# Four chained convolution blocks on one core: image 0 loaded in whole rows, weights loaded later, idle memsets left out in two images, and a new order of work

## What is computed

```python
# L0: bottleneck with a deformable convolution
mid    = relu(bn1(conv1x1(x, conv1_w)))             # 512 -> 128 channels
offset = conv3x3(mid, off_w) + off_b                # 18 channels: 9 taps, 2 coordinates
hid    = relu(bn2(deform_conv3x3(mid, offset, conv2_w)))
x      = relu(bn3(conv1x1(hid, conv3_w)) + x)       # 128 -> 512
# L1: local self correlation, 25 shifts, normalised, joined to x
corr   = l2norm(self_correlation(x, 5))
x      = relu(conv1x1(concat(x, corr), W) + b)
# L2 and L3: two plain bottlenecks 512 -> 128 -> 3x3 -> 512 with residual
```

## Time and profile before

| what | value |
|---|---|
| median of three executions | 602.6 us |
| the profiled execution's own time | 605.4 us |
| its span, from first to last instruction | 603.6 us |
| TensorE busy, share of the span | 562.2 us, 93% |
| VectorE busy | 442.3 us, 73% |
| GpSimd busy | 409.5 us, 68% |
| ScalarE busy | 327.3 us, 54% |
| mean granted TensorE clock | 0.976 of full |

### The profile page before, as it was taken

The page is one execution under the profiler, slowest core; times in us unless marked ns, Lnnn a source line. Parts: engine busy times, 40 slices in busy tenths (PEclk is TensorE's granted clock), DMA queues, the critical chain, the costliest instruction groups (busy, mean ns, idle before and its releaser), DMA issues.

```text
span 603.6 us, 8850 instructions
## 1 busy us (share of the span) xinstructions
PE 562.2 (93%) x2550; PEld 416.9 (69%) x2550; DVE 442.3 (73%) x1277; ACT 327.3 (54%) x718; POOL 409.5 (68%) x718
## 2 busy tenths in 40 slices
PE   9478986699999999799999999999999999999996
PEld 4434753576777777469777777688777776987774
DVE  3447789798988788689986788998884674463444
ACT  3445756446654874555645857654557633433534
POOL 2388888888888898888888888888787300003060
PEclk9888998899999999899999999999999999999999
DMA  8898997964568555866586557856765213000003
GB/s 307 286 355 292 276 366 222 310 186 143 160 193 296 165 150 162 280 205 171 168 264 204 168 168 251 251 159 175 223 183 148 72 59 134 0 1 1 1 1 139
DMA packets 48034, 110.08 MB, mean 182 GB/s; under 512 B 7655, under 2 KB 15911, under 8 KB 47858
## 3 DMA queue, kind: packets, MB, share of 16 engines
q0 software_dynamic: 23040, 75.52, 41.8%
q1 hardware_dynamic: 22274, 32.59, 15.6%
q10 hardware_dynamic: 2672, 1.41, 0.8%
HBM read 96.94 MB, written 12.55 MB: 181 GB/s over the span
## 4 chain that ended last, share of the span: by engine, by line
PE 71%; POOL 18%; DVE 4%; issue 3%; DMA 2%; ACT 1%; POOLq 0%; DVEq 0%; ACTq 0%
PE bank L630 16%; PE bank L632 16%; PE bank L631 16%; POOL patch L597 14%; PE bank L741 7%; POOL tick L602 4%; PE bank L749 4%; PE bank L818 4%; PE bank L730 4%; DMA patch<-patch_tables,idx_all 2%; PE bank L787 1%; PE bank L666 1%; PE bank L653 1%; DVE samp L1189 1%; DVE ring L1250 1%
## 5 line engine op out<-in xcount | busy, mean ns | idle before, releaser
L1189 DVE SCALAR_TENSOR_TENSOR samp<-patch,wgt_all,samp 128x128 f32<-128x128 f32 x864 | 240.7, 347 | 22.7 <-ACT samp L911 20.1
L597 POOL DMA_INDIRECT patch<-patch_tables,idx_all x216 | 219.8, 1017 | 40.2 <-DVE samp L1189 10.7
L911 ACT ACTIVATE samp<-patch,wgt_all 128x128 f32<-128x128 f32 x288 | 102.0, 396 | 76.4 <-DMA patch<-patch_table,idx_all 35.3
L597 POOL DMA_INDIRECT patch<-patch_table,idx_all x72 | 70.5, 980 | 30.9 <-DVE far L1086 20.3
L613 POOL TENSOR_TENSOR kept<-xs_high,xs_low 128x512 f32<-128x512 f32 x12 | 16.5, 1405 | 100.3 <-PE bank L632 100.3
L602 POOL TENSOR_TENSOR tick<-tick 1x1 f32<-1x1 f32 x288 | 79.7, 277 | 5.0
L741 PE MATMUL bank<-sampT,w 128*128 128x512 f32 x144 | 71.9, 606 | 1.5 <-ACT sampT L919 1.5
L730 PEld LDWEIGHTS bank<-ident_r,samp 128*128 128x128 f32 x288 | 35.8, 144 | 31.4 <-DVE samp L1189 16.8
L919 ACT ACTIVATE sampT<-bank 128x512 f32<-128x512 f32 x72 | 41.9, 591 | 27.8 <-PE bank L730 26.8
L730 PE MATMUL bank<-ident_r,samp 128*128 128x128 f32 x288 | 44.1, 280 | 10.5 <-DVE samp L1189 10.5
L630 PE MATMUL bank<-x_high,l1w_high 128*128 128x512 f32 x128 | 53.9, 421 | 0.0
(11 more groups left out here) (187 smaller groups left out, 1203.1 us busy)
## 6 DMA issues: line engine op xcount, KB each, us to landing
x_whole<-in_x SPq DMA_DIRECT2D x32, 256.0 KB, 7.2
out_y<-ring SPq DMA_DIRECT2D x32, 256.0 KB, 3.3
xa<-in_x SPq DMA_DIRECT2D x6, 1024.0 KB, 8.5
patch<-patch_tables,idx_all POOLq DMA_INDIRECT x216, 3.5
patch_tables<-midT SPq DMA_DIRECT2D x11, 256.0 KB, 7.1
xa<-in_x SPq DMA_DIRECT2D x8, 256.0 KB, 5.7
patch<-patch_table,idx_all POOLq DMA_INDIRECT x72, 6.0
l1w_whole<-in_l1wt SPq DMA_DIRECT2D x1, 1024.0 KB, 10.4
```

The source lines that it names most:

```text
L597: pool.indirect_dma_start(patch[:, n % SLOTS].rearrange("p a c -> p (a c)"), None, patches_n if i else patches_0, bass.IndirectOffsetOnAxi ...
L911: act.activation(samp[:, n % SAMPS, t, :], patch[:, g % SLOTS, 0, :], ACT.Copy, scale=wgt_all[:, i, (HT * h + t) * TAPS + k, 0:1]).then_in ...
L1189: dve.scalar_tensor_tensor(o_, g_, w_, o_, ALU.mult, ALU.add).then_inc(blended, 1)
```

## The change

1. **x of image 0** comes as 4 DMAs of 512 KB with whole rows of 1024 pixels, straight into x_whole, where the residual is kept. conv1 of image 0 reads it there, chunk by chunk, both halves after each other for a chunk; the 8 res loads of image 0 are gone. x of later images comes in two pieces by channel groups, and no longer by halves; image 1's is issued at once, behind image 0's.
2. **Start.** TensorE's matmuls on zeros are one of 512 and one of 256 columns, for three of 512. It waits for w1 alone, and not for the parameters too. VectorE makes its constants before it waits for the parameters.
3. **Weights.** Each waits on SP for a turn of image 0: WEIGHT_PACE gives the unit, X_PACE that of later x loads. w2 and w3 wait for image 0's table only.
4. **Pauses** are 0 in images 0 and 1, and 2 in images 2 and 3. (Before they were 0 in image 0 too.)
5. **Tables.** Each image has its own tensor in DRAM.
6. **ORDER** is a new list of 1548 steps. It differs nearly everywhere.

```diff
-PAUSE, PAUSES = 120, 2
+PAUSE, PAUSES = 120, (0, 0, 2, 2)
...
-conv1.0.0 conv1.0.1 mid.0.0 taps.0.0 mid.0.1 taps.0.2 tapped.0.0 taps.0.1 tapped.0.2 midT.0.0 tapped.0.1 midT.0.1
+conv1.0.0 conv1.0.1 mid.0.0 taps.0.0 mid.0.1 taps.0.1 tapped.0.0 taps.0.2 tapped.0.1 midT.0.1 tapped.0.2 midT.0.0
...
+WEIGHT_PACE = {7: 1, 2: 2, 3: 2, 4: 3, 5: 3, 0: 4, 1: 4, 6: 7}
+X_PACE = {2: 0, 3: 5}
...
-    table_0 = nc.dram_tensor("patch_table_0", (HW, 2 * P), fp32, kind="Internal")
-    table_n = nc.dram_tensor("patch_tables", ((N - 1) * HW, 2 * P), fp32, kind="Internal")
+    tables = [nc.dram_tensor(f"patch_table_{i}", (HW, 2 * P), fp32, kind="Internal") for i in range(N)]
...
             def load_x(i, h):
-                sp.dma_start(xa[:, :, h * HALF:(h + 1) * HALF],
-                             x_v[i, :, :, h * HALF:(h + 1) * HALF]).then_inc(ld_xa[h], 16)
+                some = slice(h * KC // 2, (h + 1) * KC // 2)
+                sp.dma_start(xa[:, some, :], x_v[i, :, some, :]).then_inc(ld_xa[h], 16)
...
+            for k in range(KC):
+                sp.dma_start(whole["x1"][:, k, PADK:PADK + H, :], grid_rows(x_v[0, :, k, :])).then_inc(ld_x0[k], 16)
             for h in range(2):
-                for k in range(KC):
-                    cols = slice(h * HALF, (h + 1) * HALF)
-                    sp.dma_start(xa[:, k, cols], x_v[0, :, k, cols]).then_inc(ld_x0[h][k], 16)
...
+                load_x(1, h)
...
+                    sp.wait_ge(conv1_done, nth(("conv1", i - 1, 0), ("conv1", i - 1, 1)))
+                    sp.wait_ge(turned, nth(("turn", 0, X_PACE[i] + h)))
                     load_x(i, h)
+                elif it[0] == "ldw":
+                    n = it[1]
+                    if n in WEIGHT_PACE:
+                        sp.wait_ge(turned, nth(("turn", 0, WEIGHT_PACE[n])))
+                    else:
+                        sp.wait_ge(tabled[0], table_dmas(0))
...
-                        for _ in range(PAUSES if i and t == HT - 1 else 0):
+                        for _ in range(PAUSES[i] if t == HT - 1 else 0):
...
             pe.wait_ge(zeroed, 1)
-            for _ in range(3):
-                pe.matmul(bank[TURN_BANK][:], w3_s[:, 0:P], w3_s[:], start=True, stop=True)
-            pe.wait_ge(ld_first, 32)
+            for n in (C, C // 2):
+                pe.matmul(bank[TURN_BANK][:, 0:n], w3_s[:, 0:P], w3_s[:, 0:n], start=True, stop=True)
+            pe.wait_ge(ld_w1, 16)
...
+                        elif h == 0:
+                            pe.wait_ge(ld_x0[c], 16)
+                            for half in range(2 if c < KC - 1 else 1):
+                                last = pe.matmul(first[half][:], w1[:, c, :], residual(half, c),
+                                                 start=c == 0, stop=c == KC - 1)
```

More of the change, by code:

```diff
@@ L44 @@
 ORDER = """
-conv1.0.0 conv1.0.1 mid.0.0 taps.0.0 mid.0.1 taps.0.2 tapped.0.0 taps.0.1 tapped.0.2 midT.0.0 tapped.0.1 midT.0.1
-pixels.0.0 shift.0 pixels.0.1 table.0.0 table.0.1 scale.0 scale.1 index.0 gather.0.0.0 hats.0 turnw.0 positions.0
-turnw.1 split.1 gather.0.0.1 split.4 split.3 split.5 gather.0.1.0 weigh.0.0.0 splitlow.5 blend.0.0.0 gather.0.1.1
-weigh.0.0.1 w3turn conv1.1.1 blend.0.0.1 xload.1.0 gather.0.2.0 weigh.0.1.0 gather.0.2.1 turn.0.0 xload.2.1 w3scale
-gather.0.3.0 split.2 mid.1.1 split.0 splitlow.0 weigh.0.1.1 sampT.0.0 blend.0.1.0 conv1.1.0 gather.0.3.1 weigh.0.2.0
@@ L65 @@
-gather.0.13.1 xsum.0.0.2 tap.0.9 positions.2 blend.0.12.0 table.3.0 res.0.1.3 res.0.1.1 out0.0.0.1 taps.3.0
-weigh.0.12.1 xsum.0.0.1 blend.0.12.1 gather.0.14.0 xhigh.0.0.0 sampT.0.11 sampT.0.10 xhigh.0.0.3 weigh.0.13.0
-xhigh.0.0.1 xlow.0.0.1 xlow.0.0.3 gather.0.14.1 xlow.0.0.0 blend.0.13.0 weigh.0.13.1 tapped.3.0 gather.0.15.0
-tapped.3.2 blend.0.13.1 shift.3 weigh.0.14.0 blend.0.14.0 gather.0.15.1 weigh.0.14.1 xhigh.0.0.2 blend.0.14.1
-gather.0.16.0 turn.0.12 tap.0.10 tap.0.11 sampT.0.12 xlow.0.0.2 weigh.0.15.0 index.3 blend.0.15.0 tap.0.12
@@ new lines @@
+pixels.0.1 shift.0 pixels.0.0 table.0.1 table.0.0 index.0 ldw.8 gather.0.0.0 hats.0 conv1.1.1 positions.0 ldw.9
+gather.0.0.1 gather.0.1.0 weigh.0.0.0 w3turn conv1.1.0 mid.1.1 blend.0.0.0 mid.1.0 gather.0.1.1 taps.1.1 taps.1.2
+tapped.1.2 weigh.0.0.1 blend.0.0.1 gather.0.2.0 turn.0.0 midT.1.1 w3scale weigh.0.1.0 midT.1.0 taps.1.0 blend.0.1.0
+gather.0.2.1 weigh.0.1.1 blend.0.1.1 gather.0.3.0 turn.0.1 weigh.0.2.0 tapped.1.0 weigh.0.2.1 sampT.0.0 blend.0.2.0
+gather.0.3.1 ldw.7 xload.2.1 pixels.1.1 sampT.0.1 tapped.1.1 blend.0.2.1 gather.0.4.0 turn.0.2 weigh.0.3.0 tap.0.0
@@ new lines @@
+ldw.2 xload.2.0 blend.0.3.0 tap.0.1 w3back shift.1 ldw.3 gather.0.4.1 weigh.0.3.1 w3s blend.0.3.1 gather.0.5.0
+weigh.0.4.0 blend.0.4.0 index.1 gather.0.5.1 weigh.0.4.1 turn.0.3 conv1.2.1 gather.0.6.0 blend.0.4.1 weigh.0.5.0
+blend.0.5.0 gather.0.6.1 ldw.4 split.4 sampT.0.2 weigh.0.5.1 blend.0.5.1 ldw.5 table.1.1 split.3 hats.1 gather.0.7.0
+turn.0.4 conv1.2.0 ldw.0 weigh.0.6.0 sampT.0.3 gather.0.7.1 mid.2.1 ldw.1 blend.0.6.0 positions.1 weigh.0.6.1 mid.2.0
+midT.2.1 tap.0.2 turn.0.5 blend.0.6.1 splitlow.3 taps.2.2 gather.0.8.0 midT.2.0 split.2 sampT.0.4 pixels.2.1
@@ new lines @@
+tapped.2.2 weigh.0.7.0 pixels.1.0 splitlow.2 turn.0.6 tap.0.3 gather.0.8.1 xload.3.0 table.1.0 weigh.0.7.1 taps.2.1
+taps.2.0 tap.0.4 blend.0.7.0 sampT.0.6 sampT.0.5 gather.0.9.0 xload.3.1 tapped.2.0 scale.1 blend.0.7.1 tapped.2.1
+split.5 pixels.2.0 weigh.0.8.0 turn.0.7 gather.0.9.1 turnw.1 shift.2 tap.0.5 ldw.6 weigh.0.8.1 scale.0 split.1
+blend.0.8.0 bias splitlow.1 gather.0.10.0 blend.0.8.1 weigh.0.9.0 sampT.0.7 blend.0.9.0 gather.0.10.1 tap.0.6 turn.0.8
+sampT.0.8 tap.0.7 index.2 splitlow.4 split.6 weigh.0.9.1 tap.0.8 conv1.3.0 gather.0.11.0 weigh.0.10.0 hid.0.0
@@ new lines @@
+blend.0.9.1 gather.0.11.1 blend.0.10.0 splitlow.6 out0.0.0.0 weigh.0.10.1 hats.2 out0.0.0.3 gather.0.12.0 turn.0.9
+turnw.0 out0.0.0.2 split.0 weigh.0.11.0 xsum.0.0.3 mid.3.0 blend.0.10.1 gather.0.12.1 xhigh.0.0.3 sampT.0.9
+weigh.0.11.1 xlow.0.0.3 xsum.0.0.2 xsum.0.0.0 conv1.3.1 midT.3.0 turn.0.10 blend.0.11.0 gather.0.13.0 weigh.0.12.0
+blend.0.11.1 corrw gather.0.13.1 blend.0.12.0 splitlow.0 turn.0.11 mid.3.1 xhigh.0.0.0 gather.0.14.0 splitlow.5
+out0.0.0.1 taps.3.0 sampT.0.10 pixels.3.0 xhigh.0.0.2 weigh.0.12.1 gather.0.14.1 taps.3.2 tap.0.9 midT.3.1 taps.3.1
@@ L450, in table_dmas @@
         def table_dmas(image):
-            return 16 * (5 if image < 2 else 4)
+            return 16 * 5
         def finals(it):
```

383 lines of the change are left out of this document (185 added, 198 removed).

## The result

The change makes the kernel slower: 607.84 us median (603.24 to 613.92, 20 runs) beside 602.84 us for the kernel before on the same chip (20 runs), ratio 1.0074 with a 95% interval of 1.0052 to 1.0096. The forecast was 597.3 us, range 593 to 603.5.

What follows compares the result with a forecast made beforehand. GpSimd's image 0 gathers bound the kernel to about 137 us, then TensorE, except a stall near 250 us. Terms −0.9 + 0.5 − 6.0 + 1.0 = −5.4 us took the profiled 605.4 to 600.0, given as a 597.3 us median, range 593 to 603.5.

Steps and rivals of the forecast that it cites:

- Start, −0.9 us: Up to the first gather: shorter zeros and earlier x let conv1 end 0.9 us sooner, bounds 0 and 1.7 us.
- rival for a cold start: conv1 begins at half clock and ends at 14.2 to 15.1 us; total 598.3 to 599.1 us; chance 0.06.
- Image 0's samples, +0.5 us: Image 0's 72 gathers: 2.6 us more VectorE work mostly fits its idle time, costing 0.5 us; GpSimd unchanged.
- The stall, −6.0 us: Near 250 us: without image 1's pauses, TensorE's 4.2 us wait and 1.8 us of half-clock loss go.
- What is late next, +1.0 us: Image 1's first third: denser VectorE work makes new waits of 1.0 us, bounds 0 and 6.
- I take 0 for the new order: Said of the tail: same chain of cvB, ex, add and store, so the new order costs 0.
- Signs: Expected profile marks; wrong if TensorE idles over 10 us after 138 us or GpSimd waits over 5 us for image 0's blends.
- The case of the other side: VectorE's queue from image 0's unit 9 on falls behind and delays TensorE; 605 to 609 us; chance 0.15.
- The stall only moves: Images 1 or 2: the new order meets another wait costing 3 to 6 us; 600.3 to 603 us; chance 0.20.

Runs made afterwards that it cites:

- h1: The change's new start and x pieces with the old list, weights at once and pauses in images 1 to 3; 615.48 us, ratio 1.0177 to the kernel before.
- h2: The change's new start and x pieces with the old list, weights at once, without image 1's pauses; 610.56 us, ratio 1.0111 to the kernel before.
- h4: The change with VectorE's splitlow subtractions replaced by one-input operations writing zeros; 607.07 us, ratio 1.0047 to the kernel before.
- k2: New start alone: old list, weights at once, later x by image halves, pauses in images 1 to 3; 602.76 us, ratio 1.0002 to the kernel before.
- f1: The change unaltered, run and profiled again; 607.51 us, ratio 1.0070 to the kernel before.
- f4: The change with the seven late weights issued at once behind image 0's x; 609.71 us, ratio 1.0096 to the kernel before.
- g4: The change without pauses in any image; 601.97 us, ratio 0.9963 to the kernel before.
- k1: New start with the old list, weights at once, later x by image halves, no pause in any image; 598.25 us, ratio 0.9915 to the kernel before.
- e1: The change with image 1's pauses back, on a chip where the kernel before took 631.05 us; 631.88 us, ratio 0.9996 to it.
- e3: The change's code with the old list, weights at once, pauses in images 1 to 3, on the slower chip; 635.73 us, ratio 1.0162 to the kernel before.
- e4: The change's code with the old list, weights at once, without image 1's pauses, on the slower chip; median 658.78 us, no ratio on record.
- g1: The kernel before, unaltered, run and profiled again; 604.84 us, ratio 1.0009 to the kernel before.
- g2: The kernel before with only image 1's pauses taken out; 598.31 us, ratio 0.9905 to the kernel before.
- h3: The kernel before without any pause; 597.69 us, ratio 0.9880 to the kernel before.

## Why the prediction was wrong

- **Start, −0.9 us.** Mis-sized, and in half of the cases with the wrong sign. Where conv1 began at the full clock, the first gather came at 22.7 to 22.9 us (after, h1, h2, h4, k2); where at the lower, at 24.6 to 25.8 us (f1 to f4, g4); k1, in between, at 23.7. (Those of e1, e3 and e4 are left out here.) The old start had 24.0 to 24.9 us. The prediction's rival for a cold start, at a chance of 0.06, had what happened in these: f1's conv1 ended at 14.4 us, within its 14.2 to 15.1. And even the early start was worth nothing to the whole (k2).
- **Image 0's samples, +0.5 us.** This is the first step that failed. It asked whether VectorE has room for 2.6 us more, and VectorE had it: GpSimd waited 0.3 us for blends in f1. The cost came through GpSimd's own durations, a gather of 1025 ns for 983: gathers stand behind operations of VectorE that read SBUF alone. "Nothing on GpSimd changes here" was true of its instructions and not of their lengths. The 72 gathers took 3.6 us more from g1 to f1, and some 2.5 on the average of four profiles of each.
- **The stall, −6.0 us.** Right: 5.7 us in g2, and image 1 is 4.7 us shorter within the change.
- **What is late next, +1.0 us.** This is the second step that failed. Beside image 1's smaller gain (4.7 for g2's 7.2 us between the two out0), images 2 and 3 were costed at nothing, "I take 0 for the new order". They cost 0.8 and 2.8 us in f1, and 2.0 and 3.6 in the first profile. The prediction says that these images "keep their pauses", as if pauses that cost nothing in the old list (h3) could cost nothing in another; in the new list taking them out shortened these images by 4.6 us (g4 beside f1). A list of 1548 steps that differs nearly everywhere was priced by the places at which I had looked.
- **Signs.** Of the two that should have told of failure one fired: TensorE is idle for 12.9 us after 138 us in the first profile and for 13.9 in f1, over the limit of 10 (before had 11.7). The other, over 5 us of waits for blends in image 0, did not: 1.1 and 0.3 us. Most of the others were missed too, the first profile first: the first gather at 22.73 and 25.11 us for 23.5 to 24.5, the last gather of image 0 at 128.6 and 131.7 for 128, out0 at 139.1 and 142.1 for 137 to 139, image 1's last gather at 237.0 and 239.8 for 236. That no wait for a blend stands in 200 to 280 us, with the clock at 1.00, came true.
- **The case of the other side** (VectorE falls behind in image 0, 0.15) had the place and not the mechanism. "The stall only moves" (0.20) came nearest: it had a new wait "in images 1 or 2, for a window step or a blend", of 3 to 6 us with its half clock, and the wait for gs and xlow is of this kind, in image 2. It stopped at 603 us, since it kept the rest of the sum.

Not settled: the new list and the new pieces of x were not run apart from each other, so what they cost without pauses, 0.84%, is shared between them. No run took VectorE's long operations away from the gathers, so their share of image 0 (3.4 us over three gathers of f1) is read from rows, and what lengthens image 1 by 2.2 us (g4 beside h3) was not looked for.

The version to keep is before without any pause (h3), 1.2% under before on a chip without the long stops; g2, which keeps the pauses of images 2 and 3, can't be told from it. h3 was not run on the chip of e1 to e4, where g2's kernel lost 2.8%.

## What to carry to other kernels

When a change replaces a whole order of work, the gain of one known stall is the safe part; price the rest by its own spread, not at zero. A filler that costs nothing in one order can lie on the critical path of another. Work moved beside a chain of another engine can lengthen that engine's instructions without making it wait, so look at mean durations as well as at waits. An idle filler should be taken out of an order that has been shown to have room; here that one edit gave 1% and the reordering around it took 1.7% back. Before a difference of one pair of profiles is explained, profile the same kernel again: identical work in image 0 differed here by up to 2.9 us.
